# A decoder layer on one core: twelve identity transposes put into each of four waits of TensorE

## What is computed

```python
x = layernorm(x + retention(x))       # scores = (q @ k.T) * gamma-decay mask; ret = scores @ v; group norm; gate
x = layernorm(x + ssm(ctx, z=x))      # conv, u = silu; state = state*exp(delta*A) + delta*u*B; y = state @ C + D*u
x = layernorm(x + ffn(x))             # silu(x1) * x3, top-2 of 8 experts, low-rank parts A/B per expert
```

## Time and profile before

| | |
|---|---|
| median of 3 runs | 442.91 us (439.5, 442.91, 442.94) |
| the profiled execution, by the same clock | 438.93 us |
| its span, first to last instruction | 437.1 us |
| TensorE matmul busy, weight load busy | 368.7 us (84%), 316.3 us (72%) |
| VectorE, ScalarE, GpSimd busy | 309.6, 186.3, 217.5 us |
| mean granted TensorE clock | 0.934 of full |

### The profile page before, as it was taken

How to read it: one execution, slowest core, us unless ns; L and a number is a source line. 1 busy time by engine, 2 the same in 40 slices (tenths; PEclk the granted TensorE clock), 3 DMA queues, 4 the chain that set the end, 5 groups by cost and what they waited for, 6 DMA issues and landing times.

```text
span 437.1 us, 6996 instructions
## 1 busy us (share of the span) xinstructions
PE 368.7 (84%) x2476; PEld 316.3 (72%) x2476; DVE 309.6 (71%) x631; ACT 186.3 (43%) x444; POOL 217.5 (50%) x223
## 2 busy tenths in 40 slices
PE   3767678669697886999989799998979999999993
PEld 2545456557565775899878688987768898899982
DVE  5476987794687599698567999856799965552223
ACT  2584534534244863452265555226555421331110
POOL 6066874967428459283045666304666631242030
PEclk9968988898686969799999999999999999999998
DMA  6491631011010232120120332011033200000000
GB/s 206 171 372 56 216 123 25 24 31 79 1 36 21 80 98 96 49 84 1 30 71 25 121 97 75 0 40 62 24 121 97 73 0 1 1 25 1 0 1 24
DMA packets 13490, 29.12 MB, mean 67 GB/s; under 512 B 1928, under 2 KB 3216, under 8 KB 13200
## 3 DMA queue, kind: packets, MB, share of 16 engines
q1 hardware_dynamic: 11584, 25.27, 17.1%
q10 hardware_dynamic: 1872, 3.41, 2.6%
HBM read 27.49 MB, written 1.18 MB: 66 GB/s over the span
## 4 chain that ended last, share of the span: by engine, by line
PE 47%; DVE 23%; issue 12%; POOL 8%; ACT 7%; DMA 1%; SPq 1%; DVEq 0%; POOLq 0%; ACTq 0%
PE xf L1060 20%; PE a2p L1060 10%; PE gen L1060 8%; PE ret L1060 5%; DVE gen L1576 4%; PE acc L1060 4%; DVE ret L1576 3%; DVE ring L1642 3%; POOL wsplit L579 2%; DVE sc L1593 2%; DVE ring L1584 2%; DVE fth L1821 2%; DMA wattn_sb<-in_wattn 1%; POOL ring L572 1%; ACT L789 1%
## 5 line engine op out<-in xcount | busy, mean ns | idle before, releaser
L1060 PE MATMUL xf<-am,wsplit 128*128 128x256 f32 x672 | 95.1, 292 | 0.5
L1060 PEld LDWEIGHTS xf<-am,wsplit 128*128 128x128 f32 x672 | 86.6, 193 | 2.7 <-DVE work L1832 1.6
L572 POOL TENSOR_TENSOR ring<-decay,brow 128x512 f32<-128x512 f32 x48 | 60.8, 1283 | 17.6 <-PE acc L1060 16.9
L683 POOL TENSOR_TENSOR work<-work,ratioT 128x256 f32<-128x256 f32 x28 | 21.7, 773 | 92.2 <-DVE work L1832 84.9
L1060 PE MATMUL a2p<-work,wff_sb 128*128 128x256 f32 x224 | 58.5, 384 | 0.5 <-POOL work L683 0.5
L1821 DVE SCALAR_TENSOR_TENSOR fth<-fth,xf 128x256 f32<-128x256 f32 x56 | 23.3, 416 | 44.6 <-ACT fth L1000 44.4
L1000 ACT ACTIVATE fth<-xf 128x256 f32<-128x256 f32 x56 | 21.1, 376 | 76.6 <-PE xf L1060 74.7
L1060 PE MATMUL acc<-ident,ring 128*128 128x128 f32 x256 | 38.7, 285 | 14.2 <-DVE ring L1584 10.2
L1060 PE MATMUL xf<-x2s,wsplit 128*128 128x256 f32 x336 | 49.7, 298 | 0.2
L1060 PEld LDWEIGHTS acc<-ident,ring 128*128 128x128 f32 x256 | 30.6, 146 | 24.1 <-DVE ring L1584 13.3
L1060 PEld LDWEIGHTS xf<-x2s,wsplit 128*128 128x128 f32 x336 | 44.0, 194 | 1.8 <-DVE work L1832 0.7
(11 more groups left out here) (308 smaller groups left out, 741.2 us busy)
## 6 DMA issues: line engine op xcount, KB each, us to landing
brow<-bc_dram SPq DMA_DIRECT2D x26, 256.0 KB, 3.5
crow<-bc_dram SPq DMA_DIRECT2D x24, 256.0 KB, 3.3
work<-in_wsp SPq DMA_DIRECT2D x3, 896.0 KB, 9.0
wff_sb<-in_wff SPq DMA_DIRECT2D x2, 896.0 KB, 7.8
am<-bc_dram SPq DMA_DIRECT2D x1, 1536.0 KB, 9.9
brow<-bc_dram ACTq DMA_DIRECT2D x6, 256.0 KB, 3.7
wattn_sb<-in_wattn SPq DMA_DIRECT2D x1, 1280.0 KB, 5.6
xT_sb<-in_xT SPq DMA_DIRECT2D x4, 256.0 KB, 3.7
```

The costliest lines, as they stand in the source:

```text
L572: pool.tensor_tensor(ring[:, i % RING], du_of(b)[:, j].unsqueeze(1).broadcast_to([P, UN, S]), brow[:, c % 2], ALU.mult).then_inc(sem["driv ...
L683: pool.tensor_tensor(xs[:, n % 4], fq[:, m % 2], ratioT[:], ALU.mult).then_inc(sem["xs_ready"], 1)
L1060: return pe.matmul(o, l, r, skip_group_check=True, **kw)
```

## The change

A helper `stay_awake(bank, turns)` transposes the identity into a 128x128 part of a bank, `turns` times, with no semaphore raised. It is called with twelve turns at the four places above, ahead of the wait there and into the bank that the waited-for work then fills. The waits around it are set in another order: in `values` the wait for `sc_ready` now stands behind the turns and behind `v_ready` (for all s and t); in `start_y` the wait for `am_ready` comes first and the one for `y_init` behind the turns; in `flip_x2(0)` a wait for `r2_ready` (the last reading of `acc`) is added ahead of the turns. What the turns write is overwritten by the work that follows. The programs of the other engines are the same.

```diff
--- before.py
+++ after.py
@@ -1083,6 +1083,11 @@
                 else:
                     need(pe, *emptied(previous(4 - m, FILLED["OUT", B - 1])))
 
+            def stay_awake(bank, turns):
+
+                for _ in range(turns):
+                    pe.transpose(bank, ident[:], ident[:])
+
             def project(s, name, w):
 
                 g = v3(gen_use(name, s), S)
@@ -1103,6 +1108,8 @@
             def low_rank(b):
 
                 g = v3(gen_use("DBL", b), S)
+                if b == 1:
+                    stay_awake(g[:, 0, 0:P], 12)
                 need(pe, "u_ready", b, 1)
                 for j in range(2):
                     last = mm(g[0:DR + 2 * DS, 0], w_xp[:, j], u[:, j], start=(j == 0), stop=(j == 1))
@@ -1152,9 +1159,11 @@
 
             def start_y(b, fb):
 
-                need(pe, "y_init", b, 2)
                 if fb is not None:
                     need(pe, "am_ready", fb, 3)
+                if b == 1:
+                    stay_awake(acc[:, 0, 0:P], 12)
+                need(pe, "y_init", b, 2)
                 for j in range(2):
                     last = flip_add(slice(j * P, (j + 1) * P), yT[:, j], j == 0, False)
                 last.then_inc(sem["y_part"], 1)
@@ -1261,11 +1270,13 @@
             def values(s, t):
 
                 o = rets[s % 2]
-                need(pe, "sc_ready", s, 4 * t + 4)
                 if t == 0:
                     if s > 1:
                         need(pe, "ro_lin", s - 2, 2)
+                    if s == 1:
+                        stay_awake(o[:, 0, 0:P], 12)
                     need(pe, "v_ready", s, 4)
+                need(pe, "sc_ready", s, 4 * t + 4)
                 for chunk in range(2):
                     cs = slice(chunk * P, (chunk + 1) * P)
                     for p_ in range(2):
@@ -1397,6 +1408,9 @@
             def flip_x2(b):
 
                 g = v3(gen_use("X2", b), S)
+                if b == 0:
+                    need(pe, "r2_ready", b, 2)
+                    stay_awake(g[:, 0, 0:P], 12)
                 need(pe, "x2_ready", b, 2)
                 for t in range(NT):
                     for k in range(2):
```

## The result

The changed kernel takes 434.41 us (median of four: 433.4, 433.88, 434.95, 437.9); the kernel before, in the four executions beside them, 441.21 us (438.17 to 442.94; three of the four are those printed ahead of the prediction). The ratio is 0.990, 95% interval 0.9851 to 0.9949. The forecast was 436.0.

A forecast was written before the change was run, and what follows sets the result against it. TensorE was taken as the busiest engine, its clock below full only in the first half. Terms 1.0 + 1.6 + 2.5 + 0 = 5.1 us, off an assumed mean of 441.1, gave 436.0 us, range 431.3 to 441.3.

The forecast's parts named there:

- A: The 2.4 us wait for the values' bias, ahead of the values of sequence 1: gain 1.0 us, bounds 0.7 and 1.65.
- B: The 2.4 us wait for x2, ahead of the value projection: gain 1.6 us, the middle of 0 and 3.1.
- C: The 2.3 us wait for u, ahead of the low-rank projection of batch 1: gain 2.5 us.
- Turns cost nothing: At all four waits: twelve turns take 1.31 us, 0.109 each, ending 0.6 us or more early at full clock.
- rival 3: Turns don't pipeline, 0.280 us each: 444.2 us if the clock isn't held, 439.1 if it is; chance of slower form 0.04.
- Turns hold the clock: At the filled waits: turns count as work, so TensorE keeps full clock; at most half its busy time is saved.
- z: TensorE's 4.5 us wait for token z, left alone: it grows longer, and the slow stretch behind it stays.
- rival 1: Turns don't count as work, the clock falls as before and nothing changes: 441.1 us; chance 0.12.
- D: The 2.1 us wait for D*u: 2.7 us saved on TensorE end in its later 4.5 us wait, gain 0.
- the upper bound of 3.1: VectorE's wait for the value projection shrinks by 1.9 us and its 1.2 us wait for the scores is gone.
- The later stages unchanged: After 181 us, where the clock was already full to 433.0 us, the profile stays as it was.
- Rival 2: Only C and A hold, and work elsewhere moves into the slow level, costing 1.65 us: 439.3 us; chance 0.12.

The follow-up runs named there:

- Z held: The change plus 36 turns in the 4.5 us wait ahead of the turning of z of batch 1; mean 433.4 us, ratio 0.9894.
- A alone: The change with only the turns ahead of the values of sequence 1, the other three calls taken out; mean 436.8 us, ratio 0.993.
- all waits: The change without turns at D, with twelve more behind x2, 36 ahead of z, and calls behind two chunk states and ahead of a variance; mean 437.3 us.
- B and D: The change with only the turns at the turning of x2 and at D*u into acc; mean 437.2 us, ratio 0.9904.
- B held: The change plus twelve more turns right behind the turning of x2, into a bank that is free there; mean 432.2 us, ratio 0.9874.

## Why the prediction was right

The total was right: 436.0 forecast, 434.41 measured, and the effect from base to result was 5.1 forecast, 5.9 +/- 3.1 by the means, or 4.6 +/- 2.0 against all later executions of the kernel before. Part of this is luck. The mean of the kernel before is 439.6 over 79 executions, and 441.1 was assumed from four. Of the terms, by the kernels with one place each, A came out larger and B and C smaller (2.8, 0.9 and 1.5 us against 1.0, 1.6 and 2.5); their sum of 5.2 lies beside 5.1 because these errors cancel, and each is known to 1.4 to 2.6 us only. That the turns themselves make the gain is clear: the change is 3.7 +/- 2.5 us under the same kernel without turns.

- **Turns cost nothing.** Right. 1.47 to 1.50 us for twelve, all over before the awaited step; 48 turns confirm 0.11 us each, and rival 3 (0.28 us) is refuted.
- **Turns hold the clock.** Right at A, C and z, in every profile that has them there, and shown by Z held more cleanly than by the rows of before; rival 1 is refuted. At B twelve turns held it in one profile of five. At D they failed in four of five: the hidden steps were to run at full speed, and their first twelve records took 2.58 us in the changed kernel's profile, against 2.93 before.
- **A, 1.0 us.** The direct saving is 1.57 us on TensorE. What reaches the end is 2.8 +/- 2.0 by A alone; the term was too small rather than too large, and its true size isn't settled. From the values at A to the projection in B the table's rows range from 57.3 to 62.9 us (all waits apart) with the falls between them, so part of A may be what it does to those.
- **B, 1.6 us.** The reason given holds: B keeps its clock in some executions. The number can't be checked: 0.9 +/- 2.6 alone. The way to the upper bound of 3.1 was wrong. VectorE's first wait shrinks to 1.5 us, but ScalarE's conv input is next, and 1.64 us is what B gives up to the variance; more comes only behind it (2.1 us up to the low-rank projection in B and D, 3.5 in B held), 1.1 us of it by the length of u. In the changed kernel's profile VectorE still waited 2.6 and 2.3 us, where the earlier trace rows had 3.3 and 1.2:

```profile
DVE vpad L1545 <- PE xf L1060: 2.6, 1, 2.6
DVE sc L1607 <- PE gen L1060: 2.3, 1, 2.3
...
DVE gavg L1770 <- PE gen L1060: 1.0, 1, 1.0
```

- **C, 2.5 us.** The size is right where the clock would fall (2.3 to 2.8 by the turns of z), and VectorE's wait for the OUT projection is gone, as said: the last row above is all that is left between 133 and 148 us. But I had counted it for every execution. In B and D the clock stayed full there without any turns, so the mean is less: 1.5 +/- 1.4 alone.
- **D, 0.** Right, though not as said: D's turns hardly held the clock, so there was little to absorb. I also expected TensorE's wait for z to grow over 4.5 us. It is 4.5 as before, and the shorter slow stretch went into a wait for a ring product before it (the row at 161.45 with 1.27 us idle ahead, which the earlier trace rows has no like of). TensorE's waits from 148 to 174 us:

```profile
PE gen L1300 <- DVE xn_sb L1797: 4.5, 1, 4.5
PE acc L1060 <- DVE ring L1598: 2.7, 2, 1.5
```

- **The later stages unchanged.** Wrong. From z to the end the profile has 262.7 us, against 261.4 before, with the two new slow stretches at 299.0 and 322.9. The waits there are old ones of 1.2 to 1.5 us. That they can let the clock go was not in my sum; all I had for it was the 2 us of spread. Nine of the thirteen profiles of changed kernels have one or two such stretches of 3.4 us, between 215 and 327 us.

Rival 2 (work moves elsewhere into the slow level) is thus partly true: the profile after has as much slow clock as the one before. In this execution, at 437.9 us, only 1.0 us of gain is left; the three others, at a mean clock of 0.947, left no profile to read.

## What to carry to other kernels

Turns of a resident identity into the bank that is next to be filled are a cheap way to keep TensorE's clock through a wait, if they can start when the wait starts: a call that itself waits for something released at the end of the stretch puts its whole length, at the lower level, on the path. Filling a few waits moves the falls about: the kernels with turns at one to six places gained 0.9 to 7.3 us, and what an execution gains depends on where its falls lie. Filling nearly all of them gave about twice the gain (10.2 against 4.6 to 5.9 us) with a scatter (standard deviation) of 0.7 us, against 2.7 of the kernel before in the same set; only Z held scattered less (0.45). Where executions of one program differ by over 1%, compare starts of the same instructions in several profiles before believing a median of a few.

## What the runs showed of the hardware

- Executions of the unchanged kernel come in groups with a granted clock of their own. In one set of 23 there were five at 436.0 to 436.4 us (clock 0.936), and six at 442.8 to 443.5 us (0.919), with the others between. The same program on the same chip, 1.6% apart.
- The fall after a given wait is not a property of the wait. With x2 turned at 111.56 us in both, the projection at 113.84 fell to the lower level in one profile and the one at 113.85 did not in another.
- 36 float32 transposes of 128x128, 0.11 us each, kept the clock at 2.4 GHz over 4.1 us without other work.
- One VectorE instruction over 128x512 float32 took 1.78 us in the six profiles where a GpSimd product began up to 0.04 us ahead of it, and 0.68 us in the eight where the product began 0.18 us or more behind it.
